# A graph attention stream with its edge features projected right behind a slot's sums, and the carried row turned first in a slot's second half

## What is computed

```python
q = (xn @ Wq + bq).reshape(n, H, DH)
k = (xn @ Wk + bk).reshape(n, H, DH)
v = (xn @ Wv + bv).reshape(n, H, DH)
ep = ef @ We + be
scores = jnp.einsum('ehd,ehd->eh', q[dst], k[src] + ep[:, None, :]) * scale
scores = scores * ew[:, None]
m = jax.ops.segment_max(scores, dst, num_segments=n)
ex = jnp.exp(scores - m[dst])
s = jax.ops.segment_sum(ex, dst, num_segments=n)
out = jax.ops.segment_sum(attn[:, :, None] * v[src], dst, num_segments=n)
```

## Time and profile before

| | us |
|---|---|
| runs | 1964.58, 1970.42, 1979.68 |
| median | 1970.42 |
| the profiled execution | 1965.13, with a span of 1963.7 |
| PE busy of it | 1643.5 (84%) |
| DVE, ACT, POOL busy | 969.5, 581.4, 794.7 |
| mean granted TensorE clock | 0.906 |

### The profile page before, as it was taken

One profiled execution on the slowest core, in us unless ns is written; L12 is line 12 of the kernel. 1 busy time (PEld: TensorE's weight loads), 2 busy tenths in 40 slices (PEclk: granted clock), 3 DMA queues, 4 the chain that ended last, 5 costly groups with the idle time before them and its releaser, 6 DMA issues.

```text
span 1963.7 us, 22797 instructions
## 1 busy us (share of the span) xinstructions
PE 1643.5 (84%) x6693; PEld 1054.4 (54%) x6693; DVE 969.5 (49%) x2256; ACT 581.4 (30%) x1373; POOL 794.7 (40%) x769
## 2 busy tenths in 40 slices
PE   5899579669799899996357889989998999899786
PEld 2455125235445455565233566767666767666575
DVE  5522242123332534344477677777667676674222
ACT  2111002122131222322122344343434444343322
POOL 1000564766766665000567545444445444430000
PEclk9899669779899899998566999999999999999898
DMA  7246453644645645111679755545545555531000
GB/s 241 118 166 222 138 145 81 174 135 133 179 139 144 191 129 171 31 60 59 196 219 280 209 147 148 148 138 149 159 142 150 143 160 147 150 92 34 19 6 8
DMA packets 191807, 270.02 MB, mean 138 GB/s; under 512 B 28564, under 2 KB 156273, under 8 KB 189105
## 3 DMA queue, kind: packets, MB, share of 16 engines
q1 hardware_dynamic: 147665, 144.74, 23.6%
q0 software_dynamic: 44000, 123.64, 22.7%
HBM read 196.22 MB, written 72.06 MB: 137 GB/s over the span
## 4 chain that ended last, share of the span: by engine, by line
PE 34%; DVE 7%; issue 4%; ACT 3%; POOL 1%; DMA 1%; SPq 1%; POOLq 0%; DVEq 0%
PE att_psR L2289 8%; PE att_psR L2316 7%; PE att_psG L2174 5%; PE att_psR L2264 4%; PE att_psR L2273 4%; POOL att_kv L1796 1%; PE att_psQ L2150 1%; PE att_psR L2250 1%; PE att_psE L2157 1%; DVE att_stat L1938 1%; PE att_psR L2308 1%; PE att_psR L2222 1%; PE att_psR L2227 1%; DVE att_n L1949 1%; PE att_psG L2173 1%
## 5 line engine op out<-in xcount | busy, mean ns | idle before, releaser
L1796 POOL DMA_INDIRECT att_kv<-table_kv,g_srcI x314 | 360.2, 1147 | 515.8 <-PE att_psG L2174 276.2
L1107 POOL DMA_INDIRECT ex_hg<-table_h,z_idx x314 | 311.3, 991 | 182.7 <-issue 86.5
L1405 PE MATMUL ex_psG<-ex_hg,ex_oh 128*42 128x256 f32 x628 | 175.6, 420 | 51.9 <-DVE ex_oh L1121 31.9
L2289 PE MATMUL att_psR<-att_t,g_mw 128*128 128x256 f32 (+1 forms) x640 | 178.1, 428 | 18.6 <-ACT att_t L2128 18.6
L2174 PE MATMUL att_psG<-att_kv,att_oh 128*42 128x264 f32 x628 | 172.3, 416 | 1.6 <-DVE att_kv L1903 0.9
L2289 PEld LDWEIGHTS att_psR<-att_t,g_mw 128*128 128x128 f32 x640 | 132.5, 215 | 46.4 <-issue 28.1
L1816 DVE TENSOR_TENSOR att_kv<-att_kv,att_epb 128x1024 f32<-128x1024 f32 x79 | 96.5, 1221 | 119.6 <-ACT att_epb L2085 82.3
L1405 PEld LDWEIGHTS ex_psG<-ex_hg,ex_oh 128*42 128x42 f32 x628 | 70.4, 126 | 155.4 <-issue 69.8
L722 PE MATMUL tab_psH<-e_u,tab_xT 128*128 128x512 f32 x320 | 146.9, 611 | 5.3 <-DVE e_u L524 5.3
L2316 PE MATMUL att_psR<-g_mw,att_h 128*128 128x256 f32 x640 | 149.2, 381 | 0.0
L2316 PEld LDWEIGHTS att_psR<-g_mw,att_h 128*128 128x128 f32 x640 | 121.8, 192 | 19.7 <-issue 3.3
(11 more groups left out here) (308 smaller groups left out, 2454.4 us busy)
## 6 DMA issues: line engine op xcount, KB each, us to landing
table_h<-tab_hs SPq DMA_DIRECT2D x20, 1024.0 KB, 3.9
att_eft<-in_eft SPq DMA_DIRECT2D x158, 64.0 KB
ex_db<-table_dst SPq DMA_DIRECT2D x79, 126.0 KB
table_ohT<-ex_ohT SPq DMA_DIRECT2D x79, 126.0 KB
att_ohT<-table_ohT SPq DMA_DIRECT2D x79, 126.0 KB
table_oh<-ex_oh SPq DMA_DIRECT2D x79, 84.0 KB
att_oh<-table_oh SPq DMA_DIRECT2D x79, 84.0 KB
ex_hg<-table_h,z_idx POOLq DMA_INDIRECT x314
```

The lines of the kernel that those rows point to most:

```text
L1107: nc.gpsimd.indirect_dma_start(hg[:, t % RING0, :], None, d.h[:, :], bass.IndirectOffsetOnAxis(ap=g.idx0[:, t:t + 1], axis=0)).then_inc(go ...
L1405: ins = nc.tensor.matmul(psG[0:WG, 0:D], oh[:, i % 3, t % TP, :], hg[:, t % RING0, :], start=(t % TP == 0), stop=last)
L1796: nc.gpsimd.indirect_dma_start(kv[:, t % (RINGC * TP), H:H + 2 * D], None, d.kv[:, :], bass.IndirectOffsetOnAxis(ap=g.srcI[:, t:t + 1], ax ...
L2289: ins = nc.tensor.matmul(out[:, c * CB:c * CB + used(b)], g.mw1[:, e, k, c * P:(c + 1) * P], t3[:, k, 0:used(b)], start=(k == 0), stop=(k ...
```

## The change

Eight edits to the order in which engines do the same work. No instruction is added or removed.

- PE: `features(i + 1)` moves from the second half of slot i, behind `queries(i + 1)`, to its first half, right behind `sums`. The wait for `in_got` moves with it from `queries` to `features`.
- PE: the scores' transpose (i % 4 == 0) moves from ahead of `sums` to behind `sums` and `features`. The two columns (i % 4 == 1), already behind `sums`, are now behind `features` too.
- PE: the carried row (i % 4 == 2) moves from the end of the second half to its start.
- ACT: the copy of psE moves from behind `scale` to right behind the copy of the sums.
- SP: `load_group(i)` waits for `q_ready` in place of `ep_made`, since `queries` now reads a buffer last.

```diff
 (ScalarE, slot_first)
                         nc.scalar.copy(part[:, j % 3, :], psG[0:WG, 0:H * VW]).then_inc(s.part_ready, 1)
+                    if i + 1 < NG:
+                        features(i + 1)
...
                         if what == "slotB":
                             if b < NG:
                                 scale(b)
-                            if b + 1 < NG:
-                                features(b + 1)
...
 (TensorE)
                 def queries(i):
-                    pe.wait_ge(in_got[i % INS], 64 * (i // INS + 1))
...
                 def features(i):
+                    pe.wait_ge(in_got[i % INS], 64 * (i // INS + 1))
...
                 def slot_first(i):
                     j = i - LAG
+                    if 0 <= j < NG:
+                        sums(j)
+                    if i + 1 < NG:
+                        features(i + 1)
                     if (n := softmax(i, 0)) is not None:
...
-                    if 0 <= j < NG:
-                        sums(j)
                     if (n := softmax(i, 1)) is not None:
...
                 def slot_second(i):
+                    j = i - LAG + 1
+                    if 0 < j < NG and j % SGG == 0:
+                        n = j // SGG
+                        pe.wait_ge(s.part_ready, j)
+                        pe.wait_ge(s.d_ready, n + 1)
+                        nc.tensor.matmul(psCarry, g.follow[0:WG, j - 1:j], part[:, (j - 1) % 3, :], start=True, stop=True).then_inc(s.carried, 1)
                     if i + 1 < NG:
                         queries(i + 1)
-                        features(i + 1)
...
-                    j = i - LAG + 1
-                    if 0 < j < NG and j % SGG == 0:
...
 (SyncE)
                 def load_group(i, features):
                     if i >= INS:
-                        sp.wait_ge(s.ep_made, i - INS + 1)
+                        sp.wait_ge(s.q_ready, i - INS + 1)
```

More of the change, by code:

```diff
@@ L2203, in slot_second @@
                         nc.tensor.transpose(psT[:, 0:P], R[:, :], g.ident[:, :]).then_inc(s.r_turned, 1)
-                    j = i - LAG + 1
-                    if 0 < j < NG and j % SGG == 0:
-                        n = j // SGG
-                        pe.wait_ge(s.part_ready, j)
-                        pe.wait_ge(s.d_ready, n + 1)
-                        nc.tensor.matmul(psCarry, g.follow[0:WG, j - 1:j], part[:, (j - 1) % 3, :], start=True, stop=True).then_inc(s.carried, 1)
                 def take(unit, b, e):
@@ L2232, in program @@
                         pe.wait_ge(g.loaded1, 16 * N_LOADED1)
+                        features(0)
                         queries(0)
-                        features(0)
                     for what, b, e in order:
```

## The result

The changed kernel took 2009.8 us (median of 4 runs, 2005.4 to 2017.1) against 1972.8 us for the kernel before (4 runs, the three given above and one more). The ratio is 1.018, with a 95% interval of 1.0146 to 1.0215, so it is slower by 29 to 42 us. I had forecast 1981.5 and a range up to 1997. On another chip, where the kernel before took 1938.3, the ratio was 1.0136 (1.0102 to 1.0171).

A forecast was written before the change was run, and what follows sets the result against it. PE was taken to bound the long part (92% busy), transfers the first part (DMA 0.82). Long part +3.8 and first part +7.3 made +11.1 on 1970.4, forecast 1981.5 us, range 1955 to 1997.

The forecast's parts named there:

- The scores' transpose: Long part: PE's wait for ACT's scaled scores goes once sums and features come first, -6.0 us.
- The carried row: Long part: DVE's list keeps the wait, and features now stand behind it, 11 places at 0.49, +5.4 us.
- So the 12.6 us stay: Long part: PE's wait for the carried row, 12.6 us in 11 places, is set by DVE's unchanged list and remains.
- ACT's copy: Long part: the features' copy delays the block's copy that PE awaits, 8 x 0.25 = +2.0 us.
- The transfers: Long part: groups issued late behind an `out` store land late for PE, 0.3 us in each of 8 blocks, +2.4 us.
- In the other slots the store and issue follow the sums at once, ... I book nothing: Long part, slots without the late issue behind an `out` store: no landing wait booked, some kept in the range.
- (c): Slot 17: block loads hold back the next group, so columns wait behind features and sums start later, +5.8 us.
- Rival 3: Slower by over 1%: the clock falls after carried-row waits, 12 us more, +23.1, 1993.5 us; or late landings, +12; chance 20%.
- (a): Very first slots: with features already copied the loop loses about 0.8 us in two of them, -1.5 us.
- (b): Slots 8, 12, 16 (transpose) and 9, 13 (columns): work now stands behind the landing, +3.0 us, bounds 0 and 15.
- part of it is made good: Slots without block work: later sums delay loads, but transfers fill 0.82, so +3.0 us was taken out of 15.
- three signs that I had named for being wrong: Carried row's wait falls by more than half, slot 17 keeps its length, or features wait in most long-part slots.

The follow-up runs named there:

- experiment 2: The kernel before with only the scores' transpose set behind the slot's sums; ratio to the kernel before 0.9979.
- experiment 1: The kernel before with only the carried row's matmul set ahead of the next slot's queries and features; ratio to the kernel before 0.9992.
- experiment 4: The changed kernel with the scores' transpose and the columns ahead of the features, still behind the sums; ratio to the kernel before 1.0073.
- experiment 5: The changed kernel with a third input buffer, each later group issued one slot sooner; ratio to the kernel before 1.0032.
- 8: Control: the kernel before with a third input buffer and no other edit; ratio to the kernel before 0.9987.
- 7: The changed kernel with transpose and columns ahead of features, a third input buffer, and features ahead of the carried row's wait inside sums; ratio to before 0.9959.

## Why the prediction was wrong

Three steps failed. Beyond what was booked, the pairs of slots with a carried row cost 12.3 us, the landings in the long part 6.0, and the slots with a transpose or columns behind a landing 5.1.

**The long part, forecast +3.8, measured +20.3.**

- *The scores' transpose*, -6.0: right. Its slots lose 7.4 us, the wait is gone. What I missed is that PE then waits for the carried row in more blocks. In experiment 2, with only the transpose moved, that wait is 5.2 us longer.
- *The carried row*: that its earlier matmul does nothing was right (experiment 1). The wait grew from 12.6 to 19.7 us (22.0 in the stretch of the earlier trace rows, forecast about 18), and behind `wo` the pairs of slots took 0.9 us more each (6.4 in 7) where I had 0.49 for the features; at most 1.7 of the 6.4 are a fall of the clock in one pair. The step that failed is "So the 12.6 us stay": I took the 11 waits as given, and the order of PE's own list decides in how many blocks PE comes early enough to wait.
- *ACT's copy*, +2.0: the wait for the block's transposed copy went from 15.0 to 15.3 us in 7 places. Too large by about 1.7.
- *The transfers*, +2.4: the wrong place. Behind the `out` store, where I booked the waits, the long part has none longer than 0.2 us. They arise in the slot behind the block loads, which takes 8.4 us more (5.9 in the second profile). The step that failed is "In the other slots the store and issue follow the sums at once, ... I book nothing". My own case (c) had shown that SP's block loads hold back the next group, and I priced it for slot 17 alone, though a block is loaded in every eight slots. Experiment 4 gives nearly all of the 8.4 back, experiment 5 all but 1.4.
- *The gates pairs*, +11.3, of which I had booked only features exposed behind the carried row, 7 x 0.49 = 3.4. By the table above 5.0 us are the wait for the carried row, 11.4 us in six pairs instead of 6.4 in four. At most 3.4 are the clock: 51.2 us at the half level instead of 44.4, and all of the difference is in the first pair. So 2.9 are left for the features and all else.
- *The clock*, not booked. In the whole long part it costs at most 6.8 us here and 10.2 in the second profile of the changed kernel. Rival 3 named it at 20% with 12 us. The size was not far off, and its other half, late landings, came as well (+6.0). The picture was wrong: the clock already fell in every block of the kernel before. The sentence of the Trainium skill that I set against this rival (TensorE: Matmul & The Clock Gate, "Why this matters for your kernels") asks for no long idle gaps between bursts of matmuls. The traces do not bear it out as enough to keep the clock. The longest gap of PE in the gates pairs is 2.27 us, before 2.14, neither of them long as that table of the Trainium skill has it, and the clock falls in all seven pairs of both kernels.

**The first part, forecast +7.3, measured +12.6.**

- *(a)*, -1.5 in the very first slots: up to queries 8 it is +1.0, but one pair of profiles does not tell. In the ten profiles that are not from the third chip these slots take 51.1 to 54.6 us in four kernels without the move of the features and 47.9 to 52.1 in six with it, so the sign may have been right.
- *(b)*, +3.0 out of bounds of 0 and 15: 8.1 us from queries 8 to 17. At the transposes (slots 8, 12 and 16) the mechanism was right to the row: scan, product, then queries, for which PE waits 1.63 us each time. At the columns of slots 9 and 13 no landing is waited for; there DVE waits 2.08 and 1.35 us for the columns behind the features. The step that failed is "part of it is made good", for which I had no row. Experiment 4 takes exactly this away.
- *(c)*, +5.8 for slot 17: +3.5. PE waits 4.54 us for the group instead of some 9, and DVE's copy of the columns comes 6.7 us later in the slot instead of 11. The features' landing in slot 17 of the changed kernel:

```profile
1107.97 1.11 PE L2157 MATMUL att_psE<-g_we,att_eft 128*128 128x64 f32 x4 [4.54 <-DMA att_eft<-in_eft]
...
1110.07 0.16 DVE L1868 COPY att_col<-att_psT 128x2 f32<-128x2 f32 x1 [6.68 <-issue]
```

**The sum.** The forecast's 11.1, and against it (a) +2.5, (b) +5.1, (c) -2.3, the landings +6.0, the pairs with a carried row +12.3 (11.3 + 6.4 measured for 5.4 booked), the transpose -1.4, ACT -2.0 (its 0.3 are inside the gates pairs), slots 4 and 5 +1.4: 32.7, for 32.9 measured from the first queries to queries 78. The range failed because I took the upper ends one at a time. The landings' terms, (b) and the slot behind the block loads, share one cause, a group that is wanted within some 5 us of its issue, and experiment 5 takes them away together. So they had to be priced together. None of the three signs that I had named for being wrong came: the wait for the carried row did not fall, slot 17 did not keep its length, and the features wait in five slots of the long part. They looked for other errors than the ones I made. Not settled is the tail behind queries 78: 5.9 us longer in one execution and 2.0 in the other, while it lasts 205.8 us in the kernel before and 208.3 and 211.6 in experiments 1 and 8, whose long part is as before. Nor is it settled why the change costs 26 us on the third chip and 35 in the first runs: there is no profile of the kernel before from the third.

## What to carry to other kernels

Before moving work that consumes a transfer to an earlier place, ask at every place of the loop how long ago its issue was, and above all which other transfers the issuing queue waits for first; if it is less than the 5 us that such a group takes here, add a buffer or leave the work where it is. On an in-order engine, put what is ready (here the transpose and the columns) ahead of what waits for a landing, so that the other engine's work lies inside the wait. And put small ready work inside a wait that exists anyway, not behind it: behind it, it lengthens the path, and here the time at the half level of the clock was longer too (experiment 5 against 7: 61.4 and 44.4 us). Before calling added busy time the clock's, add up the time at the half level in both kernels: here it was about half.

## What the runs showed of the hardware

- From the first issue of a group's four transfers to its landing took 5.5 us in the long part (1372.23 to 1377.69), with the DMA engines at 0.50. That is the upper of the two values that I had read where they are at 0.82. From the end of the last issue (1374.29) it is 3.4 us. The Trainium skill's fixed cost of about 2.0 us for one transfer (DMA: Bandwidth & Descriptors, the anatomy of one DMA) would have it, as an estimate, at 1376.3, which is 1.4 us too early here. That section gives the figure for transfers that GpSimd issues; these four are SyncE's.
- The granted clock fell for 3 to 10 us in every one of the seven gates pairs, before the change as after it, where PE has up to three or four waits of at most 2.3 us with work between them (slot 31 after: 0.57, 1.65, 1.94 and 0.54 us). Filling the wait for the carried row with zeros did not stop it. Filling the wait for ACT's copy as well did in four of seven, and then the clock fell in the slot behind the block loads in four blocks (in the changed kernel in one).
- Where the fall comes ahead of the carried row, PE is late and does not wait for it; where some of it comes behind, the pair pays for both (27.7 against 26.0 us before, 28.5 against 26.4 after).
- The long part repeats to 0.2 us, also from chip to chip: 648.2, 648.3 and 648.3 us before and in experiments 1 and 8, 668.5 and 668.3 us for the changed kernel, whose parts differ by up to 2.5 us in opposite directions. All that lies ahead of it differs far more: queries 8 start at 977 to 981 us on the third chip and at 1007 to 1023 us in all other profiles.
